# Reordering the two borders of the second attention and the tail of a fused two-layer decoder on one NeuronCore

## What is computed

```python
x = x + _L0_attn_ref(_layernorm(x), Wq, bq, Wk, bk, Wv, bv, Wo, bo)      # causal linear attention, 16 heads of 64
x = x + _L0_xattn_ref(_layernorm(x), ctx, ctx, mask, W_out)              # attention over the context, 16 heads of 16
x = x + _L0_ffn_ref(_layernorm(x), n1_w, n2_w, wq, wk, wv, wo, ...)      # causal attention, then a mixture of 4 experts
x = x + _L1_attn_ref(_layernorm(x), W_dq, W_uq, W_dkv, W_uk, W_uv, W_o)  # causal attention through a low rank
x = x + _L1_xattn_ref(_layernorm(x), ctx, ctx, q_w, q_b, k_w, ...)       # window attention over the context
x = x + _L1_ffn_ref(_layernorm(x), packed_weight, weight_scale, bias)    # rows rounded to 8 bits, ternary weights
```

## Time and profile before

| | us |
|---|---|
| median of 3 runs | 1312.16 (1310.6 to 1314.02) |
| the profiled execution, its own time | 1310.68 |
| its span in the trace | 1308.9 |
| PE busy | 1249.4 (95%), granted clock 0.991 on average |
| DVE, ACT, POOL busy | 734.5, 503.4, 281.9 |

### The profile page before, as it was taken

The page is one execution under the profiler, slowest core; times in us unless marked ns, Lnnn a source line. Parts: engine busy times, 40 slices in busy tenths (PEclk is TensorE's granted clock), DMA queues, the critical chain, the costliest instruction groups (busy, mean ns, idle before and its releaser), DMA issues.

```text
span 1308.9 us, 34635 instructions
## 1 busy us (share of the span) xinstructions
PE 1249.4 (95%) x14031; PEld 970.5 (74%) x14031; DVE 734.5 (56%) x1730; ACT 503.4 (38%) x1075; POOL 281.9 (22%) x382
## 2 busy tenths in 40 slices
PE   7999999998999999889999999999999899999995
PEld 5788777774676766557767889999998667777764
DVE  5666666665567666478864211111112666789985
ACT  2111111110555555456657333323332444444444
POOL 2000000101211211588844000000001000234532
PEclk9999999997999999999999999999999999999999
DMA  7212111110422221012200200000000000000001
GB/s 223 63 45 47 42 31 33 33 29 21 92 62 60 67 52 39 7 47 81 72 16 21 51 1 0 0 3 0 0 1 1 3 6 4 15 18 18 18 7 58
DMA packets 48480, 45.38 MB, mean 35 GB/s; under 512 B 15408, under 2 KB 44896, under 8 KB 48336
## 3 DMA queue, kind: packets, MB, share of 16 engines
q1 hardware_dynamic: 48336, 43.33, 12.7%
HBM read 39.44 MB, written 2.78 MB: 32 GB/s over the span
## 4 chain that ended last, share of the span: by engine, by line
PE 90%; issue 2%; DVE 2%; ACT 2%; DMA 1%; POOL 1%; SPq 1%; ACTq 0%; DVEq 0%
PE banks L322 51%; PE banks L826 6%; PE banks L804 4%; PE banks L985 3%; PE banks L998 3%; PE banks L315 3%; PE banks L1045 3%; PE banks L842 3%; PE banks L959 2%; PE banks L657 2%; PE banks L615 2%; PE banks L1024 2%; ACT area L1559 1%; PE banks L1040 1%; PE banks L894 1%
## 5 line engine op out<-in xcount | busy, mean ns | idle before, releaser
L1840 DVE TENSOR_REDUCE Y_room<-banks 112x2 f32<-112x750 f32 x128 | 114.2, 935 | 49.3 <-PE banks L804 49.1
L1989 DVE TENSOR_REDUCE area<-banks 112x8 f32<-112x896 f32 x96 | 100.1, 1085 | 56.3 <-PE banks L985 56.3
L1559 ACT ACTIVATE area<-banks 112x896 f32<-112x896 f32 x96 | 82.8, 914 | 111.5 <-PE banks L1045 111.5
L322 PE MATMUL banks<-room,area 128*112 128x256 f32 (+1 forms) x384 | 121.1, 467 | 3.2 <-issue 2.8
L2121 DVE SCALAR_TENSOR_TENSOR X<-banks,area,X 128x192 f32 (+1 forms) x56 | 23.3, 418 | 160.4 <-PE banks L322 160.1
L1637 ACT ACTIVATE room<-banks 128x256 f32<-128x256 f32 x123 | 47.2, 384 | 166.0 <-PE banks L322 165.9
L1446 ACT ACTIVATE area<-banks,Y_room 125x896 f32<-125x896 f32 x96 | 90.2, 1010 | 37.8 <-PE banks L826 32.9
L322 PE MATMUL banks<-area,room 128*128 128x224 f32 x512 | 103.5, 362 | 0.6 <-ACT area L1403 0.6
L322 PEld LDWEIGHTS banks<-area,room 128*128 128x128 f32 x512 | 97.8, 194 | 3.3 <-ACT area L1403 1.0
L322 PE MATMUL banks<-room,l 128*128 128x256 f32 x448 | 99.5, 379 | 0.0
L322 PEld LDWEIGHTS banks<-room,area 128*112 128x112 f32 x384 | 68.1, 183 | 40.6 <-issue 27.2
(11 more groups left out here) (237 smaller groups left out, 2417.2 us busy)
## 6 DMA issues: line engine op xcount, KB each, us to landing
area<-den_scratch SPq DMA_DIRECT2D x32, 224.0 KB, 3.6
Y_room<-in_ctx SPq DMA_DIRECT2D x16, 375.0 KB
area<-in_ctxT SPq DMA_DIRECT2D x64, 93.8 KB
area<-area SPq DMA_DIRECT2D x192, 2.6 KB
l<-in_l SPq DMA_DIRECT2D x2, 1024.0 KB, 5.4
room<-in_ctxT SPq DMA_DIRECT2D x16, 112.0 KB, 2.2
out<-X SPq DMA_DIRECT2D x16, 112.0 KB, 1.9
X<-in_x SPq DMA_DIRECT2D x1, 1568.0 KB, 17.3
```

What stands on the lines that cost most here:

```text
L322: last = nc.tensor.matmul(dst, a, w, start=(k == 0), stop=(k == len(lhs) - 1))
L1559: a_.activation(c_pT[:, i * 8 * S:(i + 1) * 8 * S].rearrange("p (j n) -> p j n", j=2), banks[0:S, 2 + 2 * i:4 + 2 * i, 0:4 * S], ACT.Exp). ...
L1840: v_.tensor_reduce(b_nb[u][:, 4 * a + k:4 * a + k + H + 1:H], banks[0:S, 2 * x:2 * x + 2, 0:SC], AX_X, ALU.max, negate=True).then_inc(Bs[" ...
L1989: v_.tensor_reduce(c_nb[:, 8 * i:8 * i + 8].rearrange("q (j n) -> q j n", j=2), banks[0:S, 2 + 2 * i:4 + 2 * i, 0:4 * S].rearrange("q j (n ...
```

## The change

Only order, queues and one bank change: no matmul, no vector operation and no DMA is added or taken away. There are six edits.

1. `weighted_a` is split into `sums_a` (the denominators) and the rest. At the start of the second attention PE's order becomes `scores_b(0, 0)`, `sums_a(15)`, `output_a(14)`, `weighted_a(15)`. `sums_a` waits for the count `den` in place of `nm`.
2. DVE takes `masked(1, 2)` and `masked(1, 3)` ahead of `normalised(14)`, and `denominators(15)` ahead of the first maxima, with `residual_a(14)` behind them.
3. SP loads the bit masks (L511 before) in step 4 of the second attention, and not ahead of the contexts 2 and 3. In its old place stands a wait for the landing of the first maxima.
4. In the three functions `second_to_third`, projections on PE, their part on ACT, and the variance, sum and row work on DVE come earlier.
5. After the mixture PE runs `to_columns(B)` ahead of `project_qk(B + 2)`.
6. Tail: `product_f(0)` runs a step earlier, in bank 0, `residual_f(0)` runs inside the last attention's loop, the residuals of all pairs move up by one, SP's twelve first stores are written out without a loop, and ACT issues the last four.

```diff
@@ SP
-            sp.dma_start(blocks_all, T["consts"][:, C_END:C_END + C_WORDS]).then_inc(ld["mask"].sem, 16)
+            sp.wait_ge(Bs["mr"].sem, Bs["mr"].at(64))
...
+                if b == QUAD:
+                    sp.dma_start(blocks_all, T["consts"][:, C_END:C_END + C_WORDS]).then_inc(ld["mask"].sem, 16)
...
-            batches(sp, stores, 1)
+            for b in range(B - LATE):
                 sp.wait_ge(Fs["xu"].sem, Fs["xu"].at(b + 1))
+                sp.dma_start(out[b], xb_(b)).then_inc(Fs["st"].sem, 16)
@@ PE
-            def weighted_a(b):
+            def sums_a(b):
 
                 pe.wait_ge(A["sm"].sem, A["sm"].at(4 * b + 4))
-                pe.wait_ge(A["nm"].sem, A["nm"].at(2 * b))
-                pe.wait_ge(A["pj"].sem, A["pj"].at(12 * (b // 2) + 10 + 2 * (b % 2)))
+                pe.wait_ge(A["den"].sem, A["den"].at(b))
...
+            def weighted_a(b):
+
+                pe.wait_ge(A["nm"].sem, A["nm"].at(2 * b))
+                pe.wait_ge(A["pj"].sem, A["pj"].at(12 * (b // 2) + 10 + 2 * (b % 2)))
...
             pe.wait_ge(Bs["qs"].sem, Bs["qs"].at(1))
-            output_a(B - 2)
             pe.wait_ge(pre["masks"].sem, 1)
             scores_b(0, 0, 0, 0)
+            sums_a(B - 1)
+            output_a(B - 2)
             weighted_a(B - 1)
...
+            def bank_f(q):
+                return pb[(2, 3, 5, 6)[q % 4] if q else 0]
...
                 if q == 0:
                     pe.wait_ge(pre["tern"].sem, 4)
+                    pe.wait_ge(W["xu"].sem, W["xu"].at(3 * B - 2))
+                if q == 1:
                     pe.wait_ge(W["ue"].sem, W["ue"].at(3 * B))
...
+                        if n == 3 * B - 2:
+                            pe.wait_ge(Fs["xu"].sem, Fs["xu"].at(2))
...
-                    if g == 3 * B + 1:
-                        product_f(0)
+                    if 3 * B <= g < 3 * B + 2:
+                        product_f(g - 3 * B)
...
+            pe.wait_ge(M["acc"].sem, M["acc"].at(ACCS * GROUPS))
+            to_columns(B)
             project_qk(B + 2)
             pe.wait_ge(W["xn"].sem, W["xn"].at(B + 4))
             pe.wait_ge(W["xte"].sem, W["xte"].at(B + 3))
             transposes(c_h, S, KT, pb[1]).then_inc(W["xt"].sem, 1)
-            pe.wait_ge(M["acc"].sem, M["acc"].at(ACCS * GROUPS))
-            to_columns(B)
@@ ACT
+            for b in range(B - LATE, B):
+                act.wait_ge(Fs["xu"].sem, Fs["xu"].at(b + 1))
+                act.dma_start(out[b], xb_(b)).then_inc(Fs["st"].sem, 16)
@@ DVE, second_to_third
                 first_rows(1)
-                phase_b(B, 0, B // 2)
                 variance_c(2)
                 sums_c(0)
                 row_c(2)
                 stats_c(3)
+                phase_b(B, 0, B // 2)
+                sums_c(1)
                 variance_c(3)
                 dve.wait_ge(Bs["pv"].sem, Bs["pv"].at(2 * B))
                 normed_c(0)
-                sums_c(1)
```

More of the change, by code:

```diff
@@ L66 @@
 UP_BANK = (1, 2, 3, 0)
+LATE = 4
 Y_SHIFT = B - 3
@@ L580, in _ @@
                     sp.dma_start(e_ctx[e % 4], src).then_inc(W[f"k{e % 4}"].sem, 16)
-            def stores(b, u, half):
-                if not on(b):
-                    return
+            for b in range(B - LATE):
                 sp.wait_ge(Fs["xu"].sem, Fs["xu"].at(b + 1))
-                sp.dma_start(out[bass.ds(b, 1)].rearrange("o s d -> (o s) d"), xb_(b)).then_inc(Fs["st"].sem, 16)
-            batches(sp, stores, 1)
+                sp.dma_start(out[b], xb_(b)).then_inc(Fs["st"].sem, 16)
             sp.wait_ge(Fs["st"].sem, Fs["st"].at(16 * B))
@@ L675, in phase_a @@
                     output_a(2 * p - 2)
+                    sums_a(2 * p - 1)
                     weighted_a(2 * p - 1)
@@ L691, in phase_a @@
                     output_a(2 * p - 1)
+                sums_a(2 * p)
                 weighted_a(2 * p)
@@ L1083, in second_to_third @@
                 weighted(n - 1, 3, (n - 1) % 2)
+                attention(0, B, -3, -2)
                 turned(n, 0, n % 4)
@@ L1088, in second_to_third @@
                 turned(n, 3, n % 4)
-                attention(0, B, -3, -2)
+                attention(0, B, -2, -1)
                 sums_t(n - 1)
@@ L1093, in second_to_third @@
                 output_t(n - 1)
-                attention(0, B, -2, -1)
+                project_qk(2)
                 for t in range(4):
@@ L1098, in second_to_third @@
                 sums_t(n)
-                project_qk(2)
                 output_t(n)
@@ L1223, in _ @@
             turned_f(2)
-            product_f(1)
             turned_f(3)
@@ L1589, in second_to_third @@
                 sums_b(n - 1)
+                squares_c(0)
+                columns_c(1)
                 for t in range(4):
                     weights(n, t, n % 2)
-                squares_c(0)
-                columns_c(1)
+                squares_c(1)
+                columns_c(2)
                 weights(n, 4, n % 2)
@@ L1596, in second_to_third @@
                 results_b(n - 1)
-                squares_c(1)
-                columns_c(2)
                 sums_b(n)
@@ L1782, in phase_a @@
                 v_of(1, 1)
+                masked(1, 2)
+                masked(1, 3)
                 if not more:
                     normalised(2 * p)
-                masked(1, 2)
-                masked(1, 3)
+                    denominators(2 * p + 1)
                 if p == 0:
@@ L1857, in _ @@
                 phase_a(p)
-            residual_a(B - 2)
             highest(0, 0, 0)
             highest(0, 1, 0)
-            denominators(B - 1)
+            residual_a(B - 2)
             v_.memset(pb[6][:, 0:4 * S], 0.0).then_inc(pre["b6"].sem, 1)
@@ L2189, in residual_f @@
                     dve.wait_ge(Fs["xb"].sem, Fs["xb"].at(n + 1))
-                    v_.scalar_tensor_tensor(xb_(n), pb[(2, 3, 5, 6)[q % 4]][0:S, i * D:(i + 1) * D], f_sc[:, n:n + 1], xb_(n),
+                    v_.scalar_tensor_tensor(xb_(n), pb[(2, 3, 5, 6)[q % 4] if q else 0][0:S, i * D:(i + 1) * D], f_sc[:, n:n + 1], xb_(n),
                                             ALU.mult, ALU.add).then_inc(Fs["xu"].sem, 1)
@@ L2210, in f_step @@
                     clipped_f(b - 10)
+                if b == 13:
+                    residual_f(0)
                 if b == 14:
@@ L2217, in _ @@
             clipped_f(4)
-            residual_f(0)
+            residual_f(1)
             f_step(B)
@@ L2222, in _ @@
                 clipped_f(q)
-                residual_f(q - 4)
-            for q in range(4, B // 2):
+                residual_f(q - 3)
+            for q in range(5, B // 2):
                 residual_f(q)
```

2 lines of the change are left out of this document (1 added, 1 removed).

## The result

| | before | changed |
|---|---|---|
| median of runs, us | 1312.98 (1310.60 to 1314.02, 4 runs) | 1295.66 (1293.48 to 1296.07, 4 runs) |
| ratio, 95% interval | | 0.9867 (0.9846 to 0.9887) |
| span of the profiled execution, us | 1308.9 | 1291.7 |
| mean granted clock in it | 0.99 | 0.99 |

The kernel is 1.3% faster. The forecast was 1295, with a span of 1291.8. That the total fits doesn't show that its terms do, so the experiments take them one by one. The ratio isn't exactly that of the two medians.

A forecast was written before the change was run, and what follows sets the result against it. PE was taken as the bound, with time to win only at borders where it idles or runs at the lower clock. 3.3 + 3.7 + 5.0 + 1.1 + 4.0 = 17.1 us, giving span 1291.8 and forecast 1295, range 1290 to 1303.

The forecast's parts named there:

- Edits 1 and 2: Start of second attention: hole before output_a(14) shrinks 2.83 to about 1.25 us, clock holds; 3.3 us, between 1.5 and 3.6.
- Edit 3: Second attention, batch 1's transposed scores: without the mask load ahead, DMA wait and slow clock go; 3.7 us, 1.0 to 4.0.
- the values: Rival at batch 1's transposed scores: values, not masks, are ahead of the maxima, so the wait stays; 1299 us, chance 0.12.
- Edit 4: Border to third stage: earlier projections and POOL block shrink PE's holes and keep the clock; 5.0 us, between 3.5 and 5.4.
- the rival of the close holes: Clock falls in holes left at 295 or near 547; price 1.7 or 1.2 us, both 2.9: 1298; chance 0.08.
- to be paid back: Border to third stage: the moved projection no longer covers DVE's normalisation, so PE waits 0.8 to 0.9 us there.
- a gain that doesn't carry: Rival: POOL's block at 559.32 starts no earlier, so the border's 5.0 us are lost in the third stage; 1300, chance 0.03.
- a third stage at the lower clock: Rival: third stage stays at the lower clock behind the border's close holes; 1338 us if for a hundred us; chance 0.03.
- Edit 5: After the mixture: a projection and its transposes fill PE's 1.17 us wait for ACT's halves; 1.1 us, between 0 and 1.2.
- Edit 6: Tail: SP's store issuing is late; earlier residuals and ACT issuing four stores gain 4.0 us, between 3.0 and 4.4.
- The rival that I made of it: Tail stays bound by transfers, eight stores in some 3.5 us; only 0.8 of 4.0 us comes; 1298, chance 0.07.
- The ten us at the lower clock: Second attention's start, PE alternating with DVE's maxima: stays as is; rival that it vanishes, 3 us more, 1292, chance 0.08.

The follow-up runs named there:

- g4: The changed kernel with the projection of batch 2 put back between the last transposed sums and the normalised output: 1292.71 us, ratio 0.9854 to the kernel before.
- f4: The changed kernel with filler matmuls in the five holes of the border to the third stage: 1293.26 us, ratio 0.9858 to the kernel before.

## Why the prediction came out right, step by step

- **Edits 1 and 2, forecast 3.3.** Right. A is 29.29 on average in the seven kernels without them and 26.00 in the seven with them: 3.3. The times give 3.0. Both halves are seen, the hole (2.83 to 1.33) and the clock behind it (5.36 to 3.71).
- **Edit 3, forecast 3.7, with 4.0 as its high end.** The mechanism was right, the size too small. B is 25.73 on average with the masks in the old place and 20.53 in the new: 5.2, and the times give 6.2. The term was taken from one execution, with a wait of 2.52 us; over seven it averages 3.7, and more clock is lost behind it (3.4 us in five of the seven, 1.7 in the other two, none with the masks moved). The range of a term that rests on a transfer's wait can't be read from one execution. That the 484 KB in front were the cause, and not the values, is shown by the kernel with only this edit.
- **Edit 4, forecast 5.0, between 3.5 and 5.4.** Right in size: at the same loss of clock, C falls from 241.6 to 237.1 (1.7 us lost), from 242.5 to 237.6 (3.4) and from 242.9 to 238.0 (5.1), so 4.5 to 5.0; the times give 5.0. In the changed kernel's own profile only 3.6 come, since the clock was worse there than before, 5.1 us lost against 1.7. That is the rival of the close holes, which I had at 0.08. It occurred in three of the five executions without fillers there, g4 with its projection included (5.1, 3.4, 1.7, against 0 and 0), and cost 0.1 to 1.0 us, not 1.2. I counted the 0.8 us "to be paid back" rightly, and g4 shows that they needn't have been paid: the projection wasn't wanted where it was moved to. The rivals of a gain that doesn't carry and of a third stage at the lower clock fell: POOL's block of 559.32 begins at 547.20, 12.1 us earlier, and the clock is at 1.00 from 552 on. The 1338 us of the second had the gain taken off twice; a hundred us at 0.6 on top of 1295 are 1355.
- **Edit 5, forecast 1.1.** From the ninth scores of the third stage to the last of all, the executions without a loss of clock in between take 693.40 to 693.64 us without it (five) and 692.21 to 692.35 with it (three): 1.2. The size came out partly by luck. Of the hole of 1.17 us that the term was made of 0.53 is left, so that it gave 0.64; the other 0.54 is the hole ahead of the projection (1008.57), which I hadn't counted. No kernel with this edit alone was run.
- **Edit 6, forecast 4.0.** Right in size, 3.9 in the tails and 3.5 by the times, and wrong in its account, which is luck. I said that SP's issuing is late, which it was, and laid the gain to ACT. It is the loop: by the traces unrolling gives 2.9 us, the moved product 1.1 to 1.3, ACT 0.1 to 0.2. I took 0.44 us for a store, from the last two of the earlier trace rows, of which the last stands behind the loop, and didn't ask at what pace the loop issues (0.73). The rule of the Trainium skill ("DMA: Bandwidth & Descriptors", "Issuing engines are not separate DMA queues") that a second issuing engine saves little agrees with this: 0.1 to 0.2 us. The rival that I made of it fails, for the stores were not bound by their transfers.
- **The ten us at the lower clock**, forecast unchanged: they stand in all fourteen profiles. They move with the work: they begin 16.1 to 17.7 us behind the end of the first attention's scores in the seven kernels without edits 1 and 2, and 12.8 to 14.3 in the seven with them, 3.3 us earlier on average, as much as A is shorter.
- **The sum.** 3.3 + 5.2 + 4.7 + 1.2 + 3.9 is 18.3, against 17.3 between the medians (14.8 to 20.2 by the interval). I had 17.1, with edit 3 short by 1.5. So the total is nearer to the forecast than its terms are, by chance within the interval. Between the two profiled executions it is 16.1 and the 1.07 of the clock at the start. I had taken the profiled execution as below the median by 1.5 us and asked no more. Its lost clock and its DMA wait were at the low end of what the same work shows, so the 1.5 us that edit 3 was short by may well be the same 1.5; that isn't shown.

**What stays open:** what makes the clock fall for ten us, 13 to 18 us behind the end of the first attention's scores, in every kernel; what decides whether it falls at the border to the third stage; and whether g4 is faster than the changed kernel by more than the 1.0 us that its trace shows at one place. The best version found is g4. f4's fillers and g4 were not combined.

## What to carry to other kernels

Before a border's idle time is costed, look at the same stretch in several executions. A hole that ends with a transfer, and the lower clock behind a hole, vary from one to the next by more than many an edit is worth (here a wait of 2.5 to 4.8 us for the same DMAs). When a queue's issues are late at the end of a kernel, look first at how far apart single issues begin while their data are ready, since a merged row of the queue holds its waits too: a loop that issues every 0.73 us what unrolled code issues every 0.49 is cheaper to mend than to share with another engine. And a gain that agrees with the forecast says nothing about its cause until the edit is taken apart.

## What the runs showed of the hardware

- The granted clock differs between executions of the same work. The stretch from `sums_t(0)` to the ninth scores of the third stage, the same code in seven kernels, lost 1.7 us of clock in three, 3.4 in two and 5.1 in two. The same five holes lost 0 in one kernel and 5.1 in another. The Trainium skill's page "TensorE: Matmul & The Clock Gate", section "Part 1: The HAM clock gate", says that the monitor's window is free-running and doesn't reset with the kernel, so that the same kernel sees another ramp in each run. The start of the program agrees (the step at 12.0 to 15.3 us, and with it 1.5 us of the time). For the falls at the border the rows show the spread and not its cause. It means that one profile can't show a hole to be harmless, as I had argued from one.
- Lost clock isn't always lost time. At the start of the second attention it is: the same product took 5.36 us behind the old hole and 3.71 behind the new. At the border to the third stage 5.1 us of it cost 1.0 us (237.99 against 237.00), where PE waits for DVE and ACT between its steps. With filler matmuls there the clock stayed at 1.00 in two profiles of two, and without them, the holes being the same, in one of four; that isn't enough to show that they keep it. They bought as little. In the alternating stretch near 308 fillers didn't keep it, with PE busy 97% of the ten us before.
- Stores that SP issues in a loop with registers begin 0.73 us apart, though each takes 0.32; unrolled they begin 0.49 apart and take 0.44. ACT's unrolled four took 1.84 us, 0.46 each.
